# A mixed-expert layer on one core: u transposed through DRAM and VectorE, bias rows added by GpSimd, expert 2 added straight from its bank

## What is computed

```python
x = x + attention(xn) + ffn(xn)

logits = xn @ router_w + router_b + load_balancer
rw = softmax(top2(logits))                       # coef, zero for the other two experts
e0 = (silu(xn @ sw_w1) * (xn @ sw_w3)) @ sw_w2
e1 = gelu(fold(xn) @ me_c1w + me_c1b) @ me_c2w + me_c2b
syn = xn @ ce_syn_w + ce_syn_b
h2 = layer_norm(syn + (syn @ ce_wv + ce_bv) @ ce_wo + ce_bo)
u  = h2 + relu(h2 @ ce_f1w + ce_f1b) @ ce_f2w + ce_f2b
e2 = layer_norm(u) @ ce_gen_w + ce_gen_b
e3 = gelu(xn @ ml_w1 + ml_b1) @ ml_w2 + ml_b2
```

## Time and profile before

| | us |
|---|---|
| median of 3 runs | 451.26 |
| lowest and highest of the 3 | 451.05 and 454.0 |
| span of the profiled execution | 449.1 |
| one turn, from one token product of TensorE to the next | 26.83 |

### The profile page before, as it was taken

The page is one execution under the profiler, slowest core; times in us unless marked ns, Lnnn a source line. Parts: engine busy times, 40 slices in busy tenths (PEclk is TensorE's granted clock), DMA queues, the critical chain, the costliest instruction groups (busy, mean ns, idle before and its releaser), DMA issues.

```text
span 449.1 us, 9603 instructions
## 1 busy us (share of the span) xinstructions
PE 438.6 (98%) x2804; PEld 371.8 (83%) x2804; DVE 402.5 (90%) x1344; ACT 271.4 (60%) x535; POOL 245.8 (55%) x366
## 2 busy tenths in 40 slices
PE   4999999999999999999999999999999999999997
PEld 3778888788888888888888988888888888888886
DVE  4887989989899898989989899898989989898897
ACT  4965838557384764838556484755838566483841
POOL 3893727557273664727466272664727466372451
PEclk9999999999999999999999999999999999999999
DMA  7522123032130412223032130413123031220201
GB/s 261 38 72 72 25 63 78 26 93 47 51 70 23 105 35 70 47 70 70 23 93 47 55 62 23 113 27 89 27 70 70 23 99 41 58 58 16 58 0 48
DMA packets 86484, 27.18 MB, mean 61 GB/s; under 512 B 64993, under 2 KB 82113, under 8 KB 86465
## 3 DMA queue, kind: packets, MB, share of 16 engines
q1 hardware_dynamic: 86176, 26.94, 25.0%
q10 hardware_dynamic: 288, 0.01, 0.0%
HBM read 14.66 MB, written 12.06 MB: 60 GB/s over the span
## 4 chain that ended last, share of the span: by engine, by line
PE 94%; DVE 3%; DMA 1%; issue 0%; DVEq 0%; ACT 0%; SPq 0%
PE S L1133 14%; PE S L1135 13%; PE S L1134 13%; PE EX L1059 12%; PE EX L1079 6%; PE S L1223 3%; PE S L1218 3%; PE S L1219 3%; PE EX L1087 3%; PE TR L1173 2%; PE S L1231 2%; PE S L1230 2%; PE S L1229 2%; PE S L1148 2%; PE S L1147 2%; PE S L1146 2%
## 5 line engine op out<-in xcount | busy, mean ns | idle before, releaser
L486 POOL TENSOR_TENSOR hid3l<-hid,hid3h 128x512 fp32r<-128x512 f32 x64 | 80.3, 1287 | 29.3 <-ACT hid3h L599 29.3
L1133 PE MATMUL S<-xh,WH 128*128 128x512 f32 x224 | 90.4, 403 | 0.0
L1135 PE MATMUL S<-xh,WL 128*128 128x512 f32 x224 | 88.4, 394 | 0.0
L1134 PE MATMUL S<-xl,WH 128*128 128x512 f32 x224 | 88.1, 393 | 0.0
L444 POOL TENSOR_TENSOR veps_x<-mv_x,eps 128x4 f32<-128x4 f32 x16 | 3.2, 200 | 111.7 <-DVE mv_x L643 111.7
L1059 PEld LDWEIGHTS EX<-scaled,hid 128*128 128x128 f32 x480 | 55.9, 192 | 1.2
L1059 PE MATMUL EX<-scaled,hid 128*128 128x128 f32 x480 | 56.0, 275 | 0.0
L1133 PEld LDWEIGHTS S<-xh,WH 128*128 128x128 f32 x224 | 42.2, 188 | 14.1 <-DVE hid L822 3.1
L1135 PEld LDWEIGHTS S<-xh,WL 128*128 128x128 f32 x224 | 42.1, 188 | 9.9
L573 ACT COPY kv<-S 128x64 f32<-128x64 f32 x64 | 13.6, 213 | 60.3 <-PE S L1148 54.6
L1134 PEld LDWEIGHTS S<-xl,WH 128*128 128x128 f32 x224 | 42.3, 189 | 8.0
(11 more groups left out here) (201 smaller groups left out, 1066.4 us busy)
## 6 DMA issues: line engine op xcount, KB each, us to landing
X<-x SPq DMA_DIRECT2D x16, 256.0 KB, 2.8
turning<-xn SPq DMA_DIRECT2D x15, 256.0 KB, 2.6
xb<-turning SPq DMA_DIRECT2D x60, 64.0 KB, 2.6
turning<-e3T SPq DMA_DIRECT2D x15, 256.0 KB, 2.4
e3b<-turning SPq DMA_DIRECT2D x60, 64.0 KB, 2.6
out<-OUT SPq DMA_DIRECT2D x15, 256.0 KB, 2.4
W<-weights SPq DMA_DIRECT2D x1, 768.0 KB, 8.2
W<-weights SPq DMA_DIRECT2D x1, 512.0 KB, 5.8
```

The source lines that it names most:

```text
L486: pool.tensor_tensor(hid3l[:, j, :], hid[3][:, j, :], hid3h[:, j, :], ALU.subtract) \
L1133: pe.matmul(bank[:, :], wh, hi, start=True, stop=False)
L1134: pe.matmul(bank[:, :], wh, lo, start=False, stop=False)
L1135: pe.matmul(bank[:, :], wl, hi, start=False, stop=True).then_inc(unit_ready, 1)
```

## The change

It has three parts.

- u is no longer transposed by TensorE, except in the last group. SyncE writes it to DRAM and brings it back in blocks into `ub`; VectorE transposes within the blocks (`u_turn`) behind silu(0) of the next turn, and takes the statistics from the result `ut` in SBUF, behind the split of K. `ub`'s four transfers stand ahead of those of e3 in the queue of SyncE.
- The two bias rows, that of expert 1 and `gen_bias` of expert 2, are no longer applied by VectorE. GpSimd makes both products with `coef`, adds them and adds the sum to `OUT`: four operations of 128x512 behind `hidl`, ahead of the `xn` of group g+2. `coef` is now made behind expert 3 of the group before, not ahead of it. Expert 0 of the next turn waits for `biases_added`, and so does expert 3 in the last turn.
- Expert 2 is added by one pass over its PSUM bank with the scalar `coef_r = coef * rstd_u` where `e<-EX` stood; the second pass over `e2` is gone. Making `coef_r` is one small instruction ahead of the routing. The store waits for expert 3.

```diff
-        turning = [nc.dram_tensor(f"turning{n}", (P, NT, P), F32, kind="Internal").ap() for n in range(2)]
+        turning = [nc.dram_tensor(f"turning{n}", (P, NT, P), F32, kind="Internal").ap() for n in range(3)]
...
                 sp.wait_ge(x_normed, g.count(NT, NT))
-                swap(g.prev(), xb, xn, turning[0], x_kept, x_swapped)
-
-            def swap_e3(g):
+                sp.dma_start(turning[0], xn[:, :, :]).then_inc(x_kept, DMA_INC)
+                sp.wait_ge(x_kept, g.prev().count(DMA_INC, DMA_INC))
+                swap_back(xb, turning[0], x_swapped)
+
+            def swap_e3_and_u(g):
+
                 b = g.bank("e3")
                 sp.wait_ge(released[b], g.uses_before("e3") + 1)
-                swap(g, e3b, e3T, turning[1], e3_kept, e3_swapped)
+                sp.dma_start(turning[1], e3T[:, :, :]).then_inc(e3_kept, DMA_INC)
+                b = g.bank("f2")
+                sp.wait_ge(released[b], g.uses_before("f2") + 1)
+                sp.dma_start(turning[2], u[:, :].rearrange("p (t n) -> p t n", t=NT)).then_inc(u_kept, DMA_INC)
+                sp.wait_ge(u_kept, g.count(DMA_INC, DMA_INC))
+                swap_back(ub, turning[2], u_swapped)
+                sp.wait_ge(e3_kept, g.count(DMA_INC, DMA_INC))
+                swap_back(e3b, turning[1], e3_swapped)
 
             def store(g):
-                sp.wait_ge(out_ready, g.count(1, 1))
+                sp.wait_ge(ex_taken[3], g.count(1, 1))
...
+            def add_biases(g, first):
+
+                if first:
+                    pool.wait_ge(bias_rows_loaded, 2 * DMA_INC)
+                    pool.wait_ge(setup_took, TAKEN.index("gen_b") + 1)
+                pool.wait_ge(att_added, g.count(1, 1))
+                pool.wait_ge(route_step, g.count(ROUTE_STEPS, ROUTE_STEPS))
+                wide = [P, NT, P]
+                pool.tensor_tensor(bias1[:, :, :], row("me_c2b").unsqueeze(1).broadcast_to(wide),
+                                   coef[g.par][:, :, 1:2].broadcast_to(wide), ALU.mult)
+                pool.tensor_tensor(bias2[:, :, :], gen_bias[:, :].unsqueeze(1).broadcast_to(wide),
+                                   coef[g.par][:, :, 2:3].broadcast_to(wide), ALU.mult)
+                pool.drain()
+                pool.tensor_tensor(bias1[:, :, :], bias1[:, :, :], bias2[:, :, :], ALU.add)
+                pool.drain()
+                ins = pool.tensor_tensor(OUT[g.par][:, :, :], OUT[g.par][:, :, :], bias1[:, :, :], ALU.add)
+                ins.then_inc(biases_added, 1)
...
-            def expert2_scale(g):
+            def expert2_coefs(g):
 
                 dve.wait_ge(u_rstd, g.count(1, 1))
+                dve.tensor_tensor(coef_r[:, :], coef[g.par][:, :, 2], rstd["u"][:, :], ALU.mult).then_inc(u_scaled, 1)
+
+            def expert2(g):
+
+                dve.wait_ge(u_scaled, g.count(1, 1))
                 dve.wait_ge(ex_ready[2], g.count(1, 1))
-                for t in range(NT):
-                    ins = dve.scalar_tensor_tensor(out=e2[:, t, :], in0=EX[EX_BANK[2]][:, t, :],
-                                                   scalar=rstd["u"][:, t:t + 1], in1=gen_bias[:, :],
+                dve.wait_ge(ex_taken[1], g.count(1, 1))
+                for t in range(NT):
+                    ins = dve.scalar_tensor_tensor(out=OUT[g.par][:, t, :], in0=EX[EX_BANK[2]][:, t, :],
+                                                   scalar=coef_r[:, t:t + 1], in1=OUT[g.par][:, t, :],
                                                    op0=ALU.mult, op1=ALU.add)
                 ins.then_inc(ex_taken[2], 1)
 
-            def expert2_add(g):
-                dve.wait_ge(ex_taken[2], g.count(1, 1))
-                dve.wait_ge(ex_taken[3], g.count(1, 1))
-                for t in range(NT):
-                    ins = dve.scalar_tensor_tensor(out=OUT[g.par][:, t, :], in0=e2[:, t, :],
-                                                   scalar=coef[g.par][:, t, 2:3], in1=OUT[g.par][:, t, :],
-                                                   op0=ALU.mult, op1=ALU.add)
-                ins.then_inc(out_ready, 1)
-
             def expert0(g):
-                mix(g, 0, bias1_added)
+                mix(g, 0, biases_added)
...
+            def u_turn(g):
+
+                dve.wait_ge(u_swapped, g.count(SWAPS * DMA_INC, SWAPS * DMA_INC))
+                dve.transpose(ut[:, :, :].rearrange("p t n -> p (t n)"), ub[:, :, :].rearrange("p t n -> p (t n)")) \
+                    .then_inc(u_whole, 1)
+
             def u_moments(g):
 
-                dve.wait_ge(u_turned, g.count(1, 1))
+                dve.wait_ge(u_whole, g.count(1, 1))
+                for t in range(NT):
+                    dve.bn_stats(stats["u"][:, t, :], ut[:, t, :])
+
...
-                if not first:
-                    u_moments(g.prev())
...
-                    u_combine(g.prev())
+                    u_turn(g.prev())
...
+                if not first:
+                    u_moments(g.prev())
+                    u_combine(g.prev())
...
                 if not first:
                     expert1(g.prev())
+                    expert2_coefs(g.prev())
...
-                    expert2_scale(g.prev())
+                    expert2(g.prev())
...
+                if first:
+                    turn_next(g)
+                if not first:
+                    mix(g.prev(), 3, ex_taken[2], src=e3t)
                 dve.wait_ge(tlean_ready, g.count(1, 1))
                 route(dve.scalar_tensor_tensor(out=coef[g.par][:, :, :], in0=tlean[:, :, :], scalar=1.0,
                                                in1=half[:, :, :], op0=ALU.add, op1=ALU.mult))
-                if first:
-                    turn_next(g)
-                if not first:
-                    mix(g.prev(), 3, ex_taken[1], src=e3t)
-                dve.wait_ge(att_added, g.count(1, 1))
-                for t in range(NT):
-                    ins = dve.scalar_tensor_tensor(out=OUT[g.par][:, t, :], in0=row("me_c2b"),
-                                                   scalar=coef[g.par][:, t, 1:2], in1=OUT[g.par][:, t, :],
-                                                   op0=ALU.mult, op1=ALU.add)
-                ins.then_inc(bias1_added, 1)
...
-                if not first:
-                    expert2_add(g.prev())
...
-                    mix(g, 3, bias1_added)
+                    mix(g, 3, biases_added)
...
-                u_moments(g)
+                last_u_moments()
                 u_combine(g)
-                dve.wait_ge(ex_taken[3], g.count(1, 1))
-                for t in range(NT):
-                    ins = dve.scalar_tensor_tensor(out=OUT[g.par][:, t, :], in0=gen_bias[:, :],
-                                                   scalar=coef[g.par][:, t, 2:3], in1=OUT[g.par][:, t, :],
-                                                   op0=ALU.mult, op1=ALU.add)
-                ins.then_inc(last_step, 1)
...
+                b = g.bank("f2")
+                pe.wait_ge(released[b], g.uses_before("f2") + 1)
...
-                    pe.wait_ge(u_read, g.prev().count(1, 1))
+                    pe.wait_ge(att_added, g.prev().count(1, 1))
...
-                b = g.bank("f2")
-                pe.wait_ge(released[b], g.uses_before("f2") + 1)
-                pe.wait_ge(att_added, g.count(1, 1))
-                for t in range(NT):
-                    ins = pe.transpose(ATT[:, t, :], u[:, t * P:(t + 1) * P], ident[:, :])
-                ins.then_inc(u_turned, 1)
                 if last:
+                    b = g.bank("f2")
+                    pe.wait_ge(released[b], g.uses_before("f2") + 1)
+                    pe.wait_ge(att_added, g.count(1, 1))
+                    for t in range(NT):
+                        ins = pe.transpose(ATT[:, t, :], u[:, t * P:(t + 1) * P], ident[:, :])
+                    ins.then_inc(u_turned, 1)
```

More of the change, by code:

```diff
@@ L193, in build @@
         e3t = sb("e3t", [P, NT, P])
+        ub = sb("ub", [P, NT, P])
+        ut = sb("ut", [P, NT, P])
+        bias1, bias2 = (sb(name, [P, NT, P]) for name in ("bias1", "bias2"))
         h2 = sb("h2", [P, T])
@@ L219, in build @@
         pr = sb("pr", [P, NT, P])
-        e2 = sb("e2", [P, NT, P])
         gate = sb("gate", [P, 4, T])
@@ L292, in build @@
         ex_taken = [sem(f"ex_taken{e}") for e in range(E)]
-        bias1_added = sem("bias1_added")
+        biases_added = sem("biases_added")
         route_step = sem("route_step")
@@ L297, in build @@
         e3_swapped = sem("e3_swapped")
+        u_kept = sem("u_kept")
+        u_swapped = sem("u_swapped")
+        u_whole = sem("u_whole")
+        u_scaled = sem("u_scaled")
         u_turned = sem("u_turned")
@@ L303, in build @@
         last_mixed = sem("last_mixed")
-        out_ready = sem("out_ready")
         def w(name, first=0, width=None):
@@ L373, in _, with swap_back @@
                     .then_inc(mask_loaded, DMA_INC)
-            def swap(g, dst, src, way, kept, done):
-                sp.dma_start(way, src[:, :, :]).then_inc(kept, DMA_INC)
```

(21 more changed lines are left out.)

2 lines of the change are left out of this document (added).

## The result

The changed kernel takes 464.85 us (median of 4 runs, 464.76 to 468.2), the one before 451.15 us on the same chip. The ratio is 1.031, with a 95% interval of 1.027 to 1.035: 3.1% slower. The forecast was 469.3 us, within 460 to 482.

The account below looks back on a forecast made before the run. TensorE was taken as full, fed by two just-in-time chains. Per turn 1.38-0.36 = +1.02 us, times 15 is +15.3; with +2.65 at the end, 449.1 becomes a 467.05 span, 469.3 us measured time, range 460 to 482.

Parts of the forecast that it names:

- pl is paced by ScalarE's copies, so an earlier VectorE gains nothing: VectorE ahead of `pl`: removing u's four statistics and their wait gives nothing, as each tile needs ScalarE's bank copy.
- Transposition, statistics and combining of u: VectorE's chain to `foundl`: transposition behind silu(0) costs 0.59 us, statistics and combining behind K cost 0.90.
- h2l's wait, -0.17: VectorE's chain to `foundl`: `h2l` waits 0.17 us for ScalarE today; VectorE arrives later, so this wait goes.
- coef_r, 0.18: VectorE's chain to `foundl`: the new small instruction costs 0.18 us with its gap.
- The product, 1.38 later: TensorE's product needing `foundl`: starts at T+15.20 against T+13.82, T being the token product's start; 15 turns lose 1.38 us each.
- TensorE gains 0.36 a turn: TensorE ahead of the next token product: the four transposes of u leave 15 of 16 groups, 0.36 us each.
- GpSimd, 5.45 for the biases, n1 0.65 late, hidden: GpSimd: four new operations take 5.45 us; `n1` starts 0.65 late, hidden inside TensorE's wait for `foundl`, cover 0.8 us.
- The DMA in time: u's return through DRAM: back at T+4.0 to 4.6, wanted at T+5.6; cost 0, cover about 1 us.
- VectorE's savings behind foundl are worth nothing: VectorE behind `foundl`: eight instructions, about 2.1 us a turn, go; it idles until the next `pl`, so costed at 0.
- The end, +2.65: Last turn: expert 3 waits for GpSimd's biases, 2.65 us later; the removed tail adds were hidden, gain 0.
- two chains that are just in time: TensorE's inputs: VectorE's `foundl` for the product and GpSimd's `n1` for its transposes, both starting with TensorE's token product.
- no later part of TensorE's order gives the loss back: TensorE behind the product: the 1.38 us lost per turn stays, because the next token product follows TensorE itself.

Follow-up runs that it names:

- E1: The changed kernel with `foundl` moved ahead of `coef_r` and the five routing steps, straight behind expert 1: 476.56 us, ratio 1.058 to the kernel before.
- E5: The changed kernel with u transposed by TensorE as before, leaving biases on GpSimd and expert 2 straight from its bank: 461.45 us, ratio 1.020 to the kernel before.
- E6: The kernel before with only u sent through DRAM and VectorE; biases and expert 2 stay on VectorE: 491.69 us, ratio 1.087 to the kernel before.
- E11: E6 with the store of `OUT` placed behind u and e3 in SyncE's queue: 462.16 us, ratio 1.026 to the kernel before.
- E8: E1 with `coef_r` made by GpSimd behind `rstd_u` instead of VectorE: 460.32 us, ratio 1.020 to the kernel before.
- E3: The changed kernel with `foundl` straight behind expert 1 and `coef` straight behind silu(2): 492.17 us, ratio 1.091 to the kernel before.

## Why the prediction was right

The forecast was 4% slower and the result is 3.1%; the mechanism is the one forecast, and no rival came in. Point by point:

- **pl is paced by ScalarE's copies, so an earlier VectorE gains nothing.** Right: `stats_c` at T+2.06 in both kernels, and 45.1 us of waiting ahead of `pl`, 2.9 a turn ("2 to 3").
- **Transposition, statistics and combining of u, 1.49.** Right: expert 0 went from T+6.75 to T+8.25, 1.50.
- **h2l's wait, -0.17.** It gave 0.26: from `pr` to `h2l` are 0.59 us now (242.66 to 243.25), where there were 0.85.
- **coef_r, 0.18.** It advances VectorE by 246.27-246.20 = 0.07. So `foundl` is 1.50-0.26+0.07 = 1.31 later, by its own rows 1.32, where 1.50 were forecast. The 0.07 is no property of the instruction: E1 and E5 show 1.18 and 0.60 for it. The prediction didn't ask what GpSimd does at that moment; that its 0.18 was enough is luck.
- **The product, 1.38 later.** It is 1.16 later. `foundl` ends at 247.82 and the product starts at 247.88, so the signal takes 0.06, not 0.1, and 0.16 of the 0.22 between the two rows was spare. This and the two lines above are the mis-sized terms (`h2l` by 0.09, `coef_r` by 0.11, the signal by 0.04, up to rounding): 0.22 a turn, 3.3 us, of the 4.05 by which the forecast span (467.05) lies above the measured 463.0. The rest is the end, below.
- **TensorE gains 0.36 a turn.** 0.37.
- **GpSimd, 5.45 for the biases, n1 0.65 late, hidden.** From 255.71 to 260.55 they take 4.84: the two with broadcast operands 1.05 each, less than the 1.27 of a plain one, where I had put 1.27 to 1.74. Of the 0.65 by which n1 was to be late they save 0.61: the factor of the next n1 starts at 236.36, T+3.46, as before, and the shorter wait of TensorE for n1, one of the signs I named, did not come. But GpSimd's idle 0.63 ahead of it is used up, so this chain is just in time too. The 2.6 cycles per element that the Trainium skill (GPSIMD Engine Reference, section 3.1) states for two inputs make no difference between operands, and from them the prediction took 1287 ns for these too. The measurement decides: for 512 elements per partition, with one input a row repeated over the four tiles and the other a number held over each 128, it is 1050.
- **The DMA in time.** Right, VectorE doesn't wait: the last return of u is issued near 261.4 and lands 2.6 later, T+3.5, and VectorE comes to it at T+5.4, a cover of 1.9 us. (The prediction had u back at foundl+17.0 to 17.7; the terms that it gives add up to 16.5 to 17.2, and 16.5 is measured.) But the sentence "Cost 0, with a cover of about 1 us" didn't name what the cover hung on: the store ahead of u in the queue. E6 shows its price where the store is late, 29 us of span against E11, some 5 of them the lower clock.
- **VectorE's savings behind foundl are worth nothing.** Right: it idles 2.9 us ahead of `pl` instead.
- **The end, +2.65.** +2.0, for the cheaper biases. The last turn (VectorE, then GpSimd):

```profile
448.53 0.17 DVE L964 SCALAR_TENSOR_TENSOR coef<-tlean,half 128x16 f32<-128x16 f32 x1
...
453.82 1.13 DVE L784 SCALAR_TENSOR_TENSOR OUT<-EX,coef,OUT 128x128 f32<-128x128 f32 x4 [3.56 <-POOL OUT L524]
```

```profile
452.45 1.27 POOL L524 TENSOR_TENSOR OUT<-OUT,bias 128x512 f32<-128x512 f32 x1
```

What the prediction lacked though its number held: it spoke of "two chains that are just in time" and there are three. It also wrote that no later part of TensorE's order gives the loss back, without asking whether a later part would take it anew; the release of e3's bank by VectorE, 0.3 us from being late, does. Whoever had repaired the change by moving `foundl` forward alone, as E1 does, would have found the loss again 3.5 us later in the turn.

One thing stays open. In the changed kernel the meeting of `h2l` and the first `hid3l` falls on GpSimd (2.1 us instead of 1.29), in E6 mostly on VectorE (`h2l` 1.06 in the mean instead of 0.68), though `hid3l` starts first in both, by 0.24 and by 0.73 us. Which side yields was read from the rows but not tested.

## What to carry to other kernels

When a saving is made on an engine that is already ahead, look for where its added work stands against the consumer that is just in time, and then for the next such consumer behind it: undoing one bound gains only what separates it from the second. An instruction's length can depend on what another engine does at that moment, so one that moves by a microsecond has to be looked up again where it lands. Longer isn't yet slower: `coef_r` at 1.18 us stood on TensorE's path and cost 16 us (E1, E8), four adds at 2.80 stood ahead of idle time and cost nothing in that turn (E3). A transfer leaves when everything ahead of it in its queue may leave, so a wait that is put into a store is put into all transfers behind it.

## What the runs showed of the hardware that was not expected

- A VectorE instruction with both inputs in SBUF and a `tensor_tensor` of GpSimd hold each other up. In these meetings the one that starts while the other runs lasts until about the end of the running instruction, whatever its own size: `coef_r`, 128x4, 0.15 alone and 1.18 in E1, where a `hid3l` of 1.27 had just begun; 0.60 in E5, where half of one was left; `h2l` 1.09 in E6, where it starts 0.73 us behind a `hid3l`. Four adds of `e3t` took 2.80 instead of 1.14 (E3). It also goes the other way too. In the changed kernel `h2l` starts 0.24 us behind the first of four `hid3l` (243.25 against 243.01) and keeps its 0.68, and the `hid3l` is the longer one:

```profile
L499 POOL TENSOR_TENSOR hid3l<-hid,hid3h x64: 1267/1286/2146, 25.1 to 441.1; 128x512 fp32r<-128x512 f32 x64
```

  The median is 1286 ns, the longest 2146; the mean is 1467, where it was 1287 before. So the starts in a trace don't yet tell which side pays. VectorE's adds with one input in PSUM, such as those of expert 2 in E1 (four at 255.08, 1.12 us, while `hidl` runs), keep their length. The Trainium skill (GPSIMD Engine Reference, section 8, Key points) names such contention for VectorE instructions with two inputs in SBUF; the runs agree, and give it the size that it has here: where it falls on the later one, what is left of the other engine's running instruction.
- A GpSimd `tensor_tensor` of 128x512 that multiplies two broadcast inputs takes 1050 ns, one that adds two plain ones 1268, in all kernels with the biases where no VectorE instruction is in its way. Whether it's one broadcast, both or the product that makes it shorter, no run shows.
- From VectorE's recorded end of `foundl` (247.82) to TensorE's start of the product (247.88) the signal took 0.06 us.
